# The low halves of q reach the attention operand by DMA, and the preparation of the weights is rewritten

## The chip, the cores and the metric

The kernel runs on one core of one Trainium2 chip. Its time is the device time of one execution in microseconds (us). The engines named below are TensorE (PE, with its weight loads as PEld), VectorE (DVE), ScalarE (ACT), GpSimd (POOL) and SyncE (SP), whose queue issues all DMAs here. A granted clock of 1.00 for TensorE means 2.4 GHz and 0.50 means 1.2 GHz.

## What is computed

The input x is 32 x 256 tokens of 128 numbers. Cut to what matters:

```python
q = relu((x @ Wq)) * SCALE; k = relu(x @ Wk); v = x @ Wv      # 64 heads of 64
kv    = einsum('bsid,bsjd->bsdj', k, v)
out   = einsum('bsid,bsdj->bsij', q, kv)
norm  = einsum('bsid,bsd->bsi', q, k.sum(axis=2))
x     = layernorm(x + (out / (norm + 1e-6)).reshape(b, s, 4096) @ Wo + bo)
h     = silu(fp4(x) @ fp4(w_gate).T) * (fp4(x) @ fp4(w_up).T)   # 352 wide
x     = layernorm(x + fp4(h) @ fp4(w_down).T)
```

`fp4` scales each block of 16 numbers by its largest magnitude over 6 and rounds to the grid 0, 0.5, 1, 1.5, 2, 3, 4, 6. In every token `kv` is summed over the same 64 heads for which `out` is taken, so the kernel needs, for each token, the sum of k over the heads and a 64 x 64 product of q with v.

## The kernel before

The 8192 tokens are worked in 64 tiles of 128. Matrix products are made of bf16 pairs: a float32 operand is split in a high half (its bf16 rounding) and a low half (what remains), and `three` adds high x high, high x low and low x high in PSUM. The high halves are written by ScalarE (`v_hi`, `q_hi`, `o_hi`), the low halves by VectorE (`v_lo`) and GpSimd (`q_lo`, `o_lo`).

There are 68 turns. In turn n the engines work on five tiles at once: the front (v, k and q of tile n), attention (`attend`, tile n-1), the output projection (`mid`, tile n-2), the first layernorm and gate/up (`back`, tile n-3), and the second layernorm (`end`, tile n-4). Each engine has its own order for a turn, written out by hand in `iteration(t)`, and engines meet only at semaphores. There is no scheduler: an instruction that waits holds up all that stands behind it on its engine.

TensorE's turn is: v 0 and 1, v 2 and 3, `x_transpose`, k 0 to 2, `h_transpose`, k 3, `down`, q 0, out 0, `k_sum`, out 1, `xq_transpose`, `gate_up`, q 1, out 2 and 3, q 2, out 4 and 5, output projection (`wo_part`, L408) 0 and 1, q 3, out 6, `wo_part` 2, out 7, `wo_part` 3 and 4. A chunk of v, k or q is 24 matmuls of 128 columns, an out group 24 of 66 columns. Three slots in PSUM of two banks each hold the chunks in the order of use (`USES`, `SLOT`); `wait_slot` lets a chunk in once its slot's earlier tenant has been read. By this order q 0 waits until VectorE has read k 1, and k 2 until it has read v 3.

`q_nat` holds q as it comes from VectorE (`q_scale`) with high and low halves; `q_bd` is the attention operand, block-diagonal, with two halves of 64 partitions for two parities. For each half (l = 0 high, l = 1 low) there are four blocks of 64 partitions x 2048 bf16: two change partitions and go by DMA (`q_move`), two stay on theirs (`q_stay`). Before, ScalarE copies three of those that stay (L563: the low one of partitions 0 to 63, and both high ones), and GpSimd the fourth (L1090, a multiplication by 1 from `consts`: the low one of partitions 64 to 127). All must be there before out 0:

```python
pe.wait_ge(s_qstay, t.n * 3)
pe.wait_ge(s_qstay_p, t.n)
pe.wait_ge(s_qbd, t.n * 64)
pe.wait_ge(s_vswap, t.n * 48)
```

SP's queue carries, per turn, three moves for the tile's o (`swap<-o_st`, `o_st<-o_st`, `o_st<-swap`, 512 KB each), three for its v (576 KB each), the four `q_move`s (256 KB each) and three small transfers. `wo_part(0)` waits for the last of the o moves.

After the tile's k has been summed over its chunks on VectorE (`k_add`, then three halvings `k_fold`, L733), `k_sum` (L447) on TensorE folds partitions, ScalarE copies the result to `ks`, and `q_scale` 0 starts from that. Between the second and the third `k_fold` VectorE has `norm_o(0)`, which waits for out 0. GpSimd's turn: `rstd_1` (two small operations for the first layernorm, L1067 and L1069), `q_stay`, `x_back`, `rstd_2`, then `q_lo` (L1051) 0 to 3 between `o_lo` (L1061) 0 to 7, `x_bias` and `h_back`. `x_one` (L820) on VectorE normalises with the result of `rstd_1`; it reads r1 and rs1, both in SBUF.

Ahead of the turns VectorE quantises w_gate and w_up (88 partitions x 1024) and w_down (128 x 352) by comparisons with the seven midpoints, and writes the low half of Wq (L708); GpSimd writes the low halves of Wv, Wk (L1030) and Wo (L1036).

## Time and profile before

| | |
|---|---|
| median of 3 runs | 2490.99 us (2480.89 to 2496.33) |
| the profiled execution | 2491.44 us, span 2489.7 us |
| mean granted TensorE clock | 0.941 |
| PE / PEld busy | 86% / 81% |
| DVE busy | 84% |
| POOL busy | 68% |
| ACT busy | 60% |
| DMA (mean of 16 engines) | 56.5% for the kernel's queue, 302.65 MB |

The profiled execution's own time is 0.45 us above the median, and 1.7 us of it lie outside the span. No engine is full, and the busy shares hardly change over the length of the run, so what limits the kernel is in how one turn closes on the next.

### The profile page before, as it was taken

The numbers are of one execution on the slowest core, as the hardware profiler recorded it, in microseconds if no ns is written. First come the engines' busy times: TensorE is split into PE (matmuls) and PEld (weight loads), VectorE is DVE, ScalarE is ACT, GpSimd is POOL, SyncE is SP. The second block draws the span as 40 slices with busy tenths as digits, with TensorE's granted clock in tenths as the row PEclk, the third lists the DMA queues.
The fourth block names the chain that finished last, engine by engine and source line by source line (L and its number), as shares of the span: only waits on it lengthen the run. The fifth ranks groups of instructions, "written<-read, shape, count | busy, mean of one in ns | idle before, by whom it ended". The sixth has DMA issues, their size and how long they took to land.

```text
span 2489.7 us, 88190 instructions
## 1 busy us (share of the span) xinstructions
PE 2144.2 (86%) x37963; PEld 2015.4 (81%) x37963; DVE 2088.1 (84%) x3943; ACT 1483.3 (60%) x2634; POOL 1702.6 (68%) x2068
## 2 busy tenths in 40 slices
PE   1788988988988988888898898898898898898875
PEld 1787978888888888888888888888888798898874
DVE  8679888888888888888888888888888988888874
ACT  3556656656656656656666666665665665665651
POOL 6566766766776776776776676676676676676673
PEclk9899999999999999999999999999999999999986
DMA  4456556556556556556656656655645655655651
GB/s 147 103 122 143 112 121 138 121 117 145 121 116 142 120 115 141 123 113 140 129 113 134 130 114 133 133 117 126 147 105 124 135 114 126 146 110 121 147 109 41
DMA packets 523211, 308.28 MB, mean 124 GB/s; under 512 B 275590, under 2 KB 497734, under 8 KB 522310
## 3 DMA queue, kind: packets, MB, share of 16 engines
q1 hardware_dynamic: 522822, 302.65, 56.5%
q8 instruction: 298, 4.88, 0.8%
q14 instruction: 91, 0.75, 0.1%
HBM read 17.38 MB, written 4.19 MB: 9 GB/s over the span
## 4 chain that ended last, share of the span: by engine, by line
PE 47%; DVE 32%; issue 10%; POOL 5%; ACT 5%; DMA 1%; SPq 0%; DVEq 0%; POOLq 0%; ACTq 0%
PE ps L408 13%; PE ps L361 10%; PE ps L362 9%; PE ps L363 9%; DVE k_acc L722 9%; DVE v_st L740 9%; DVE k_acc L733 3%; PE ps L462 3%; POOL o_st L1061 3%; POOL q_nat L1051 3%; ACT v_st L539 2%; PE ps L463 2%; DVE q L757 2%; PE ps L447 1%; DVE o L781 1%
## 5 line engine op out<-in xcount | busy, mean ns | idle before, releaser
L1061 POOL TENSOR_TENSOR o_st<-o,o_st 128x256 bf16<-128x256 f32 x1024 | 662.3, 680 | 50.9 <-ACT o_st L622 50.1
L1051 POOL TENSOR_TENSOR q_nat<-q,q_nat 128x512 bf16<-128x512 f32 x512 | 590.5, 1175 | 89.2 <-ACT q_nat L598 89.2
L622 ACT CAST o_st<-o 128x256 bf16<-128x256 f32 x1024 | 352.6, 403 | 285.2 <-DVE o L781 281.9
L361 PE MATMUL ps<-v_st,q_bd 128*128 128x66 bf16 x4096 | 465.9, 201 | 51.8 <-DVE o L781 25.1
L361 PEld LDWEIGHTS ps<-v_st,q_bd 128*128 128x128 bf16 x4096 | 423.4, 115 | 77.6 <-DVE o L781 41.4
L362 PE MATMUL ps<-v_st,q_bd 128*128 128x66 bf16 x4096 | 461.5, 200 | 0.0
L363 PE MATMUL ps<-v_st,q_bd 128*128 128x66 bf16 x4096 | 460.2, 199 | 0.0
L362 PEld LDWEIGHTS ps<-v_st,q_bd 128*128 128x128 bf16 x4096 | 424.8, 117 | 1.5 <-issue 0.4
L363 PEld LDWEIGHTS ps<-v_st,q_bd 128*128 128x128 bf16 x4096 | 422.3, 116 | 0.0
L598 ACT CAST q_nat<-q 128x512 bf16<-128x512 f32 x512 | 292.0, 618 | 210.6 <-DVE q L757 210.4
L361 PE MATMUL ps<-xT,w_q 128*128 128x128 bf16 x2048 | 377.5, 226 | 45.9 <-DVE k_acc L722 40.0
L408 PE MATMUL ps<-w_o,o_st 128*128 128x128 bf16 x6144 | 376.3, 220 | 4.0 <-DMA o_st<-swap 4.0
L362 PE MATMUL ps<-xT,w_q 128*128 128x128 bf16 x2048 | 374.9, 225 | 0.0
L363 PE MATMUL ps<-xT,w_q 128*128 128x128 bf16 x2048 | 373.0, 225 | 0.0
L757 DVE SCALAR_TENSOR_TENSOR q<-ps,ks 128x1024 f32<-128x1024 f32 x256 | 309.0, 1207 | 72.8 <-PE ps L363 55.8
L563 ACT COPY q_bd<-q_nat 64x2048 bf16<-64x2048 bf16 x192 | 363.6, 1894 | 7.7 <-POOL q_nat L1051 4.6
L361 PE MATMUL ps<-xT,w_v 128*128 128x128 bf16 x2048 | 351.4, 221 | 14.0 <-DVE v_st L740 12.2
L781 DVE TENSOR_TENSOR o<-ps,rec 128x512 f32<-128x512 f32 x512 | 337.4, 683 | 28.3 <-POOL o_st L1061 19.5
L740 DVE TENSOR_TENSOR v_st<-ps,v_st 128x1024 bf16<-128x1024 f32 x256 | 312.6, 1222 | 54.4 <-ACT v_st L539 45.1
L408 PEld LDWEIGHTS ps<-w_o,o_st 128*128 128x128 bf16 x6144 | 351.8, 114 | 5.0 <-DMA o_st<-swap 5.0
L362 PE MATMUL ps<-xT,w_v 128*128 128x128 bf16 x2048 | 351.3, 221 | 0.0
L363 PE MATMUL ps<-xT,w_v 128*128 128x128 bf16 x2048 | 351.3, 221 | 0.0
(133 smaller groups left out, 5710.0 us busy)
## 6 DMA issues: line engine op xcount, KB each, us to landing
q_bd<-q_nat SPq DMA_DIRECT2D x256, 256.0 KB, 3.9
swap<-v_st SPq DMA_DIRECT2D x64, 576.0 KB, 6.5
v_st<-v_st SPq DMA_DIRECT2D x64, 576.0 KB, 5.2
v_st<-swap SPq DMA_DIRECT2D x64, 576.0 KB, 5.4
swap<-o_st SPq DMA_DIRECT2D x64, 512.0 KB, 4.4
o_st<-o_st SPq DMA_DIRECT2D x64, 512.0 KB, 8.3
o_st<-swap SPq DMA_DIRECT2D x64, 512.0 KB, 5.9
x_in<-in_L_attn_x SPq DMA_DIRECT2D x64, 64.0 KB, 5.4
```

Of the source, the lines that this page charges most:

```text
L361: nc.tensor.matmul(dst, lhs(0), rhs(0), start=True, stop=False)
L362: nc.tensor.matmul(dst, lhs(0), rhs(1), start=False, stop=False)
L363: return nc.tensor.matmul(dst, lhs(1), rhs(0), start=False, stop=True)
L408: last = nc.tensor.matmul(Y, omat[t.par][:, lo, j // EB, :, j % EB], womat[:, lw, j, :], start=(j == 0 and k == 0), stop=(j == HALF - 1 an ...
L563: nc.scalar.copy(qbd[rows, l, :, a, e:e + HALF, :].rearrange("p k e s -> p k (e s)"), qnat[rows, l, a].rearrange("p k e s -> p k (e s)")). ...
L598: last = nc.scalar.copy(qnat[:, 0, a, :, c * EC:(c + 1) * EC, :], src[:, a])
L622: last = nc.scalar.copy(ost[1 - t.par][:, 0, :, a, g * G:(g + 1) * G, :], src[:, a])
L740: nc.vector.tensor_tensor(lo, slot_cols(("v", c)).rearrange("p e t -> p t e"), hi, ALU.subtract).then_inc(s_read["v"], 1)
L757: nc.vector.scalar_tensor_tensor(out=q32[:, c % QR, :].rearrange("p (e t) -> p e t", t=T), in0=slot_cols(("q", c)), scalar=0.0, in1=ks[:, ...
L781: nc.vector.tensor_tensor(o32[:, g % OR, :].rearrange("p (s b e) -> p s b e", b=2, e=HALF), slot_cols(("out", g))[:, :, 0:PW].rearrange("p ...
L1051: last = nc.gpsimd.tensor_tensor(qnat[:, 1, a, :, e, :], src[:, a], qnat[:, 0, a, :, e, :], ALU.subtract)
L1061: last = nc.gpsimd.tensor_tensor(lo[:, :, a], src[:, a], hi[:, :, a], ALU.subtract)
```

## The change

Both low blocks of q that stay now go by DMA, in a new `q_stay` on SP's queue, right behind the two low `q_move`s; ScalarE keeps the two high ones, and GpSimd has none. Out 0 waits for six transfers instead of four. The orders of the engines are edited in some places: on VectorE the first layernorm's statistics stand ahead of `v_lo(0)`, `x_one` ahead of `v_lo(3)`, `x_lo` behind `k_add(2)`, and `norm_o(6)` and `h_round` change places around `q_scale(3)`; on GpSimd `h_back` stands ahead of `o_lo(7)`; on ScalarE `h_step` stands three steps earlier.

The preparation: gate and up weights are quantised by the rounding trick that x and h already use (nine VectorE operations in place of sixteen), the low halves of Wv and Wk are written by VectorE, the quantising of w_down moves to the end of VectorE's turn 0 (its transposes and copies to turn 1), and the split of Wo moves into turn 0 (ScalarE behind `k_first`, GpSimd behind all that it has to do ahead of the first `q_lo`).

```diff
@@ sync @@
+            sp.dma_start(x_in[:, :], x_t[0:T, :]).then_inc(s_x, 16)
             for g, w in enumerate((w_gate, w_up)):
                 sp.dma_start(gu[0:WP, g], w.rearrange("(q p) k -> p q k", p=WP)).then_inc(s_fload, 16)
-            sp.dma_start(dn_raw, w_down).then_inc(s_fload, 16)
-            sp.dma_start(x_in[:, :], x_t[0:T, :]).then_inc(s_x, 16)
...
+            sp.dma_start(dn_raw, w_down).then_inc(s_dload, 16)
...
+            def q_stay(l, par):
+
+                rows, e = slice(par * 64, par * 64 + 64), par * HALF
+                sp.dma_start(qbd[rows, l, :, par, e:e + HALF, :].rearrange("p k e s -> p k (e s)"),
+                             qnat[rows, l, par].rearrange("p k e s -> p k (e s)")).then_inc(s_qbd, 16)
...
                     q_move(1, 0)
                     q_move(1, 1)
+                    q_stay(1, 0)
+                    q_stay(1, 1)
@@ tensor @@
-                    pe.wait_ge(s_qstay, t.n * 3)
-                    pe.wait_ge(s_qstay_p, t.n)
-                    pe.wait_ge(s_qbd, t.n * 64)
+                    pe.wait_ge(s_qstay, t.n * 2)
+                    pe.wait_ge(s_qbd, t.n * 96)
@@ scalar @@
-                q_stay(t, 1, 0)
+                if t.is_(0):
+                    weight_o_hi()
                 hq_copy(t)
-                q_stay(t, 0, 1)
-                q_stay(t, 0, 0)
+                q_stay(t, 1)
+                q_stay(t, 0)
                 k_sums(t)
+                if t.is_(1):
+                    down_weights()
...
                 o_hi(t, 4)
+                h_step(t)
                 o_hi(t, 5)
                 q_hi(t, 3)
                 o_hi(t, 6)
-                h_step(t)
                 o_hi(t, 7)
@@ vector @@
+            def quantise(raw, q, np_):
+                nb, w = raw.shape[1] // BLK, raw.shape[1]
+                raw, q, sc, rs = raw[0:np_], q[0:np_], w_sc[0:np_, 0:nb], w_sc[0:np_, 64:64 + nb]
                 link(nc.vector.tensor_reduce(sc, blocks(raw), AX.X, ALU.max, apply_absolute_value=True))
                 link(nc.vector.tensor_scalar(sc, sc, 1.0 / 6.0, 1e-12, ALU.mult, ALU.max))
                 link(nc.vector.reciprocal(rs, sc))
...
+                link(nc.vector.scalar_tensor_tensor(out=blocks(raw), in0=blocks(raw), scalar=BELOW_ONE,
+                                                    in1=per_block(rs, raw), op0=ALU.mult, op1=ALU.mult))
...
+                link(nc.vector.tensor_tensor(raw, q, raw, ALU.add))
+                link(nc.vector.tensor_tensor(q, raw, q, ALU.subtract))
                 nc.vector.tensor_tensor(blocks(q), blocks(q), per_block(sc, raw), ALU.mult).then_inc(s_wquant, 1)
...
+            for k in "vkq":
+                dve.wait_ge(s_whi[k], 1)
...
             def iteration(t):
                 residual_1(t)
-                v_lo(t, 0)
-                v_lo(t, 1)
                 stats_1(t)
                 before_mean_1(t)
+                v_lo(t, 0)
+                mean_1(t)
+                v_lo(t, 1)
                 v_lo(t, 2)
-                mean_1(t)
+                x_one(t)
                 v_lo(t, 3)
-                x_one(t)
                 k_add(t, 1)
                 x_max(t)
+                k_add(t, 2)
                 x_lo(t)
                 x_scale(t)
-                k_add(t, 2)
+                k_add(t, 3)
                 x_recip(t)
-                k_add(t, 3)
...
                 scale_o(t, 7)
-                h_round(t)
-                h_grid(t)
+                if t.is_(0):
+                    down_quantise()
@@ gpsimd @@
-            for k in "vk":
-                pool.wait_ge(s_whi[k], 1)
...
+            pool.wait_ge(s_whi["o"], 1)
+            nc.gpsimd.tensor_tensor(w_o[:, 1, :], stage["o"], w_o[:, 0, :], ALU.subtract).then_inc(s_wlo["o"], 1)
             pool.wait_ge(s_store, 16)
...
                 rstd_1(t)
-                q_stay(t)
                 x_back(t)
...
                 o_lo(t, 6)
+                h_back(t)
                 o_lo(t, 7)
-                h_back(t)
                 q_lo(t, 3)
```

GpSimd, from the last low half of q in one turn to the first in the next, before. `ve` and `rs` are `rstd_1` and `rstd_2`, `xq` is `x_back`.

```order
L1109 TENSOR_TENSOR h<-h,hsc 128x352
L1051 TENSOR_TENSOR q_nat<-q,q_nat 128x16x32 x2
L1067 TENSOR_TENSOR ve<-mv,consts 128x1
L1069 TENSOR_TENSOR rs<-ve,consts 128x1
L1090 TENSOR_TENSOR q_bd<-q_nat,consts 64x16x128
L1103 TENSOR_TENSOR xq<-xq,xsc 128x128
```

The same place after the change:

```order
L1072 TENSOR_TENSOR o_st<-o,o_st 128x8x32 x2
L1104 TENSOR_TENSOR h<-h,hsc 128x352
L1072 TENSOR_TENSOR o_st<-o,o_st 128x8x32 x2
L1062 TENSOR_TENSOR q_nat<-q,q_nat 128x16x32 x2
L1078 TENSOR_TENSOR ve<-mv,consts 128x1
L1080 TENSOR_TENSOR rs<-ve,consts 128x1
L1098 TENSOR_TENSOR xq<-xq,xsc 128x128
```

The operation on q_bd between `rs` and `xq` is gone, and `h` has moved up by one o_lo.

SP's queue at the start of a turn, before:

```order
L286 DMA swap<-o_st 64x16x256
L291 DMA q_bd<-q_nat 64x16x128 x2
L286 DMA swap<-v_st 64x2x2304
L286 DMA o_st<-o_st 64x16x256
L286 DMA v_st<-v_st 64x2x2304
L286 DMA o_st<-swap 64x16x256
```

And after:

```order
L285 DMA swap<-o_st 64x16x256
L290 DMA q_bd<-q_nat 64x16x128 x2
L296 DMA q_bd<-q_nat 64x16x128 x2
L285 DMA swap<-v_st 64x2x2304
L285 DMA o_st<-o_st 64x16x256
L285 DMA v_st<-v_st 64x2x2304
L285 DMA o_st<-swap 64x16x256
```

Two transfers of 256 KB now stand ahead of four of the moves of v and o.

VectorE at the start of a turn, before: the residual, the four `v_lo` (`v_st<-ps,v_st`) with the statistics between them, `x_one`, and the first `k_add`.

```order
L802 TENSOR_TENSOR r<-ps,x_res 128x128
L740 TENSOR_TENSOR v_st<-ps,v_st 128x128x8 x2
L807 BN_STATS st<-r 128x6
L740 TENSOR_TENSOR v_st<-ps,v_st 128x128x8
L815 BN_AGGR mv<-st 128x2
L740 TENSOR_TENSOR v_st<-ps,v_st 128x128x8
L820 SCALAR_TENSOR_TENSOR x<-r,mv,rs 128x128
L722 SCALAR_TENSOR_TENSOR k_acc<-ps,k_acc 128x1024
```

And after:

```order
L817 TENSOR_TENSOR r<-ps,x_res 128x128
L822 BN_STATS st<-r 128x6
L755 TENSOR_TENSOR v_st<-ps,v_st 128x128x8
L830 BN_AGGR mv<-st 128x2
L755 TENSOR_TENSOR v_st<-ps,v_st 128x128x8 x2
L835 SCALAR_TENSOR_TENSOR x<-r,mv,rs 128x128
L755 TENSOR_TENSOR v_st<-ps,v_st 128x128x8
L737 SCALAR_TENSOR_TENSOR k_acc<-ps,k_acc 128x1024
```

The normalisation `x` now stands ahead of the last `v_lo`.

## Rows read from the trace of the kernel before

**Rows 1.** The page, the chain that ended last: share of the span.

```profile
PE 47%; DVE 32%; issue 10%; POOL 5%; ACT 5%; DMA 1%; SPq 0%; DVEq 0%; POOLq 0%; ACTq 0%
```

**Rows 2.** The waits, whole run: us in total, times, longest.

```profile
PE ps L447 <- DVE k_acc L733: 134.0, 64, 2.6
```

**Rows 3.** The line L447: min/median/max ns, first and last start.

```profile
L447 PE MATMUL ps<-k_acc,both x128: 275/377/583, 69.7 to 2393.6; 128*128 128x128 f32 x128
```

**Rows 4.** ScalarE in order of time, ks of turn 2.

```profile
131.92 0.27 ACT L576 COPY ks<-ps 128x128 f32<-128x128 f32 x1 [2.02 <-PE ps L447]
```

**Rows 5.** VectorE in order of time, two turns: start, us, what.

```profile
1235.08 3.77 DVE L820 SCALAR_TENSOR_TENSOR x<-r,mv,rs 128x128 f32<-128x128 f32 x1
...
1271.88 3.77 DVE L820 SCALAR_TENSOR_TENSOR x<-r,mv,rs 128x128 f32<-128x128 f32 x1
```

**Rows 6.** Groups by line, whole run: busy us, mean ns | idle.

```profile
L820 DVE SCALAR_TENSOR_TENSOR x<-r,mv,rs 128x128 f32<-128x128 f32 x64 | 227.4, 3554 | 6.8 <-POOL rs L1069 6.8
```

**Rows 7.** GpSimd in order of time, the same turn.

```profile
1230.86 2.29 POOL L1051 TENSOR_TENSOR q_nat<-q,q_nat 128x512 bf16<-128x512 f32 x2
...
1234.38 0.55 POOL L1069 TENSOR_TENSOR rs<-ve,consts 128x1 f32<-128x1 f32 x1
1235.10 3.60 POOL L1090 TENSOR_TENSOR q_bd<-q_nat,consts 64x2048 bf16<-64x2048 bf16 x1 [0.17 <-POOL rs L1069]
...
1248.37 2.27 POOL L1051 TENSOR_TENSOR q_nat<-q,q_nat 128x512 bf16<-128x512 f32 x2 [0.24 <-ACT q_nat L598]
```

**Rows 8.** ScalarE in order of time, the same turn.

```profile
1237.36 0.59 ACT L570 COPY hqT<-ps 128x128 f32<-128x128 f32 x3 [0.21 <-PE ps L429]
1237.98 3.82 ACT L563 COPY q_bd<-q_nat 64x2048 bf16<-64x2048 bf16 x2
```

**Rows 9.** TensorE in order of time, the same turn.

```profile
1227.33 0.22 PE L361 MATMUL ps<-xT,w_v 128*128 128x128 bf16 x1
...
1241.85 0.22 PE L361 MATMUL ps<-v_st,q_bd 128*128 128x66 bf16 x1 [0.30 <-ACT q_bd L563]
...
1245.02 0.49 PE L447 MATMUL ps<-k_acc,both 128*128 128x128 f32 x2 [2.17 <-DVE k_acc L733]
...
1255.79 1.90 PE L408 MATMUL ps<-w_o,o_st 128*128 128x128 bf16 x31
```

**Rows 10.** One us: busy PE, PEld, DVE, ACT, POOL; clock; DMA, GB/s.

```profile
1246.00:1247.00 1.00, 0.88 (x13) 0.58 (x10) 1.00 (x2) 0.09 (x2) 0.04 (x1) 0.50 0.97 187
```

**Rows 11.** SP's queue in order of time, the same turn.

```profile
1233.17 1.31 SPq L291 DMA_DIRECT2D q_bd<-q_nat  x2
...
1243.58 0.59 SPq L286 DMA_DIRECT2D o_st<-swap  x1
```

**Rows 12.** DMA issues, 1225 to 1275 us: KB, us to landing.

```profile
o_st<-swap SPq DMA_DIRECT2D x1, 512.0 KB, 6.0
```

**Rows 13.** VectorE in order of time, the last turn with attention.

```profile
2419.97 0.35 DVE L820 SCALAR_TENSOR_TENSOR x<-r,mv,rs 128x128 f32<-128x128 f32 x1 [4.05 <-POOL rs L1069]
```

**Rows 14.** SP's queue in order of time, the end of turn 0.

```profile
82.68 3.93 SPq L291 DMA_DIRECT2D q_bd<-q_nat  x4
```

**Rows 15.** Stretches of 0.5 us there: clock, DMA share, GB/s.

```profile
84.00:84.50 0.50, 1.00 0.90 199
...
88.50:89.00 0.50, 1.00 0.84 172
```

**Rows 16.** VectorE in order of time, preparation.

```profile
8.57 1.22 DVE L687 TENSOR_TENSOR v_st<-v_st,o_st 88x1024 f32<-88x1024 f32 x1
...
13.78 11.22 DVE L693 SCALAR_TENSOR_TENSOR v_st<-v_st 88x1024 f32<-88x1024 f32 x3
...
57.29 3.49 DVE L740 TENSOR_TENSOR v_st<-ps,v_st 128x1024 bf16<-128x1024 f32 x3
```

**Rows 17.** GpSimd in order of time, preparation.

```profile
46.33 8.78 POOL L1036 TENSOR_TENSOR w_o<-q_nat,w_o 128x4096 bf16<-128x4096 f32 x1 [6.82 <-ACT w_o L524]
```

**Rows 18.** DMA issues, first 62 us: KB, us to landing.

```profile
v_st<-in_L_attn_Wq SPq DMA_DIRECT2D x1, 2048.0 KB, 17.6
```

More of the change, by code:

```diff
@@ L616, in o_hi @@
                     return
+                if g == 0 and t.is_(2):
+                    act.wait_ge(s_wlo["o"], 1)
                 if g == 0 and t.back:
@@ new lines, in quantise @@
+                nc.vector.tensor_tensor(blocks(q), blocks(q), per_block(sc, raw), ALU.mult).then_inc(s_wquant, 1)
+            dve.wait_ge(s_fload, 32)
+            quantise(gu_raw, gu_q, WP)
+            dve.wait_ge(s_xhi, 1)
+            nc.vector.tensor_tensor(xT[0][:, 1, :], TB1[:, 0:T], xT[0][:, 0, :], ALU.subtract).then_inc(s_xlo, 1)
+            for k in "vkq":
+                dve.wait_ge(s_whi[k], 1)
+                for hh in range(2):
+                    hi, lo = (wmat[k][:, l].rearrange("p e (h m) -> p e h m", h=2)[:, :, hh] for l in range(2))
+                    if k == "q":
+                        last = nc.vector.scalar_tensor_tensor(out=lo, in0=split_src["q"][:, :, hh], scalar=SCALE, in1=hi,
+                                                              op0=ALU.mult, op1=ALU.subtract)
+                    else:
+                        last = nc.vector.tensor_tensor(lo, split_src[k][:, :, hh], hi, ALU.subtract)
+                last.then_inc(s_wlo[k], 1)
@@ L996, in iteration @@
                 y(t)
-                norm_o(t, 6)
                 scale_o(t, 5)
                 q_scale(t, 3)
+                h_round(t)
+                norm_o(t, 6)
                 norm_o(t, 7)
```

105 lines of the change are left out of this document (32 added, 73 removed).

## The prediction

> **What bounds the kernel now.** I read the chain of work that ended last first [rows 1]: 47% of the span is TensorE, 32% VectorE, and 10% "issue", time in which an engine waited for nothing that the profile shows. The waits then name where the two engines meet: before `k_sum` TensorE stands 134.0 us in 64 turns for VectorE's last `k_fold` [rows 2]. `k_sum` is therefore the clock of a turn. Its first start is 69.7 us and its last 2393.6 us [rows 3]; that of turn 2 lies half a microsecond ahead of the ScalarE copy that reads it, at 131.4 us [rows 4]. From there to the last, 61 turns take 2262 us, 37.08 us each. The two turns shown are 36.80 us apart (1271.88 less 1235.08) [rows 5].
>
> Why VectorE is late stands in the same rows: `x_one`, 128 x 128, takes 3.77 us [rows 5]. Over the run it has a mean of 3554 ns [rows 6], against 0.35 us in the last turn with attention, where it came ahead of GpSimd's copy [rows 13]. In the ordinary turn GpSimd's q_stay starts at 1235.10 us, 0.02 us behind `x_one`, and ends at 1238.70; `x_one` ends 0.15 us after that [rows 5, 7]. So VectorE stands still for 3.4 us in each turn while GpSimd copies from SBUF. The Trainium skill, page "SBUF — State Buffer", section "SBUF: two separate sides", says that a VectorE operation with two SBUF inputs and a GpSimd operation take a shared pair of ports as an exclusive lock. By that rule the copy holds `x_one` for its whole length, and the trace agrees.
>
> Then the clock: behind the 2.17 us of idling before `k_sum` [rows 9] TensorE's granted clock is 0.50, its 1.2 GHz level, in the microsecond from 1246 us [rows 10]. A mean of 0.941 for the run means that 0.118 of the time, 4.4 us a turn, is spent at that level; half of it, 2.2 us, is lost to TensorE. I take 1.7 for this turn.
>
> **The change in the steady turn.** I count from a `k_sum`, at 0.
>
> GpSimd's q_stay (3.60 us) goes. Nothing of GpSimd waits behind it that is urgent, so the gain is `x_one`: 3.77 to 0.35 us, 3.4 us off VectorE's path to the next `k_sum`. If nothing else were late, the turn would be 33.4 us.
>
> What is late next, on four paths:
>
> (a) GpSimd. Its first `q_lo` starts at 3.35 (1248.37 less 1245.02) and its last ends at 24.9 (1230.86 + 2.29 + 36.80, less 1245.02) [rows 7, 9]. In between it works nearly without a gap, and the change takes nothing from that stretch; `h_back` moves within it. I take 24.7. `rstd_1` stands behind it and takes 0.8 (its second part ends at 1234.93) [rows 7]; before, this was hidden, since `x_one` came behind all four `v_lo`. Now `x_one` stands ahead of `v_lo(3)`, so the chain is: 24.7, `rstd_1` 25.6, `x_one` 25.95, `v_lo(3)` with its 1024 columns (1.22 us each, the starts a little closer) [rows 16] 27.1. k 2 needs the slot that this frees. Behind k 2 come `h_transpose` (together 1.8 us), `hq_copy` 0.6, and ScalarE's two high copies, 3.82 us [rows 8]: 33.3. Out 0 starts then, takes 1.0, and `norm_o(0)` and the last `k_fold` 0.5 more: the next `k_sum` at 34.9.
>
> (b) ScalarE. It loses one copy of 1.9 us, but that one lay in its wait for `h_transpose`; the other two still start right behind `hq_copy`, as before at 1237.98 [rows 8]. From v 0 to the end of the copies are 14.5 us (1227.33 to 1241.80) [rows 8, 9]. So the removed copy is worth nothing, and TensorE's wait for ScalarE before out 0 (0.30 us in this turn) becomes longer, since q 0 comes earlier. v 0 starts at 19.1 after the `k_sum` now (1227.33 + 36.80 less 1245.02), and at 17.4 if the clock stays up: the next `k_sum` by this path at 35.1 or 33.4.
>
> (c) The low halves by DMA. SP issues the two moves at 1233.17, as GpSimd ends, 1.31 us for both [rows 11]. Now it issues four. Four moves of this size in a row stand at the end of turn 0: issued from 82.68, their data flows from 84.0 to 89.2, so 1.3 us each and 6.5 us in all [rows 14, 15]. From 24.7 that gives 31.2, ahead of ScalarE's 33.3. Two fewer waits on engines, one longer on the DMA, 2.1 us of cover.
>
> (d) The moves behind them in the queue. v's and o's moves come later by the two added transfers, 2.6 us. The last of o is issued at 35.4 (1243.58 + 36.80 less 1245.02) and takes 6.0 [rows 11, 12]: 41.4, then 44.0. `wo_part(0)` reads it 10.8 after the next `k_sum` [rows 9], so at 47.6 before, and at 45.7 now, or 44.2 with the clock up. A margin of 6.2 us shrinks to 0.2 to 1.7.
>
> The cost of the added transfers can be seen in another way. The Trainium skill, page "DMA: Bandwidth & Descriptors", section "Specifications", asks for at least 512 bytes per piece for full rate; these pieces are 256 bytes, so by it each move costs about twice its bytes, some 2.6 us as an estimate. The sum of (d) would then be 46.6, and the o moves would be the bound. What the trace has for pieces of this size speaks against it: 199 and 172 GB/s in [rows 15]. I take 1.3 us each, with 2.1 as the upper bound.
>
> I take 34.9 us for the turn, from (a), with (b) at 33.4 to 35.1 beside it. 61 turns give 61 x (37.08 - 34.9) = 133 us. Turn 2 has no `x_one` but three copies on ScalarE in a row; it loses one, 2 us. The last turn with attention has the short `x_one` already and gains nothing.
>
> **The preparation.** VectorE's first `v_lo` is at 57.29 us [rows 16]. Now the gate and up weights take seven operations of 1024 columns at 1.22 us, two small ones of 0.4, from about 5 us on: 14.6, with x 14.9. The old ones of this size took 3.7 each where GpSimd split Wv and Wk beside them (11.22 us for three) [rows 16]; GpSimd has nothing there now. Six operations of 2048 columns follow, at twice 1.22 or less: 29.5. Wq lands at 3.5 + 17.6 = 21.1 [rows 18] and ScalarE needs 3.6 for it, which gives 24.7 and with the last two 29.6. So 27.7 us come forward. From that goes what is put into turn 0: the split of Wo, 8.78 us on GpSimd [rows 17], now falls on `k_fold`, which reads SBUF on both inputs, so between 0 and 7 us. I take 6, since ScalarE's copy of Wo ends about where `k_fold` begins. The quantising of w_down (seven operations of 352 columns, some 0.5 us each by 1.22 x 352/1024 and the fixed part) goes ahead of turn 1's `v_lo`, which had 2 us of idling: 3.5, up to 7 if `q_lo` blocks it. 27.7 - 6 - 3.5 = 18 (14 to 26). The small edits (`norm_o(6)` behind `q_scale(3)`, `h_step` earlier, `x_lo` later) I cost at nothing: they move idling of VectorE within the second half of the turn, where GpSimd sets the pace; were they on the path, 0.3 us a turn either way.
>
> The sum against the profiled execution: 2491.4 - 133 - 2 - 18 = **2338 us**. It is 0.45 us above the median of the runs, so the same number stands for the median.
>
> **The rivals.**
>
> TensorE sets the pace. If the clock stays up and `rstd_1` comes sooner than I think, path (b) gives 33.4 to 33.6: 61 x 3.55 = 217, and with 20 for the rest **2254 us**. For it: the chain is mostly TensorE. Against it: GpSimd's stretch is full.
>
> The DMA sets the pace. With 2.1 us for each added move the o moves land at 45.6 and `wo_part(0)` waits: 45.6 - 9.6 = 36.0 a turn, 66 us less and 20 for the rest, **2405 us**. For it: the queue carries them in front of four larger moves, and the margin is small. Against it: the rate in [rows 15].
>
> Slower. The same mechanism at a higher price: a copy whose source and destination are the same 64 partitions has no row of this size alone. If the two cost 8 us together, o lands at 49.4 and the turn is 38.6: 61 x 1.5 = 93 more, less 20, **2564 us**. It decides from 6.9 us for both (41.4 + 6.9 - 10.8 = 37.5). Nothing in the rows is that slow.
>
> It doesn't do what it says. If `x_one` is slow for another reason than GpSimd's copy, 3.5 us stay, and only the preparation is won: about **2470 us**. Against it: [rows 13].
>
> **How the numbers follow.** My forecast has 0.62, TensorE's pace 0.15, the DMA's 0.15, slower 0.04, nothing but preparation 0.04. The forecast's own range is 2289 to 2387 (34.1 to 35.7 a turn). To hold 8 in 10 it must reach to both neighbours: 2250 to 2410. Faster by over 1% (about what a measurement of this kernel can tell from no change) takes in the first three, 0.92; within 1% 0.05, slower by over 1% 0.03.
>
> **What would show it.** `x_one` at 0.35 us in all turns; TensorE's wait before `k_sum` under 1 us a turn, and a longer one before out 0 that ScalarE ends, not a DMA; a short wait of k 2 for `v_lo(3)`; mean granted clock over 0.941; the last move of o landing 2 to 3 us later in the turn, with no wait of `wo_part`; the first `v_lo` near 30 us and a `k_fold` of some us in turn 0. I am wrong if TensorE's idling is short and a turn is under 34 us, or if `wo_part` or out 0 waits for a DMA.

## The result, and the profile after

The changed kernel takes 2428.84 us (median of 4 runs, 2424.65 to 2429.46), the kernel before 2493.66 us (4 runs, 2480.89 to 2498.93). The ratio is 0.9744, with a 95% interval of 0.9704 to 0.9784: 2.6% faster, where 6% was forecast, and above the range. The profiled execution took 2429.46 us, 62 us less than that of before; its span is 2427.7 us and its mean granted clock 0.946 (before 0.941).

The chain that ended last, on the page of after:

```profile
PE 51%; POOL 13%; ACT 12%; DVE 9%; DMA 7%; issue 5%; SPq 2%; ACTq 0%; DVEq 0%; POOLq 0%
```

Against [rows 1], VectorE's share has gone from 32% to 9%, as it had to if `x_one` was the brake. But 7% of the chain is now DMA, of which [rows 1] had 1%.

TensorE's waits after, over the run (us in total, times, longest us):

```profile
PE ps L368 <- issue: 60.0, 21, 9.8
PE ps L368 <- ACT q_bd L571: 52.8, 42, 2.1
PE ps L368 <- DVE o L796: 47.0, 89, 2.6
PE ps L451 <- DVE k_acc L748: 37.2, 64, 8.4
...
PE ps L414 <- DMA o_st<-swap: 16.2, 13, 6.0
```

The wait before `k_sum` fell from 134.0 us [rows 2] to 37.2, 8.4 of them in turn 0. In its place TensorE waits ahead of out 0 (L368 is the first matmul of chunks and out groups): 42 times for ScalarE's copies, which was foreseen, and 21 times for "issue", which is a wait that the trace gives no engine for. What ends these is shown below. The longest of the 21, 9.8 us, is out 0 of the last turn with attention.

VectorE's normalisations after, by line (busy us, mean ns):

```profile
L905 DVE SCALAR_TENSOR_TENSOR y_out<-r,mv,rs 128x128 f32<-128x128 f32 x64 | 92.1, 1439 | 0.9 <-POOL rs L1080 0.9
L835 DVE SCALAR_TENSOR_TENSOR x<-r,mv,rs 128x128 f32<-128x128 f32 x64 | 22.4, 350 | 19.3 <-POOL rs L1080 13.6
```

`x_one` has a mean of 350 ns where [rows 6] had 3554: the stall is gone in all 64 turns. Still, `k_sum` gives only this (min/median/max ns, first and last start):

```profile
L451 PE MATMUL ps<-k_acc,both x128: 275/377/582, 51.0 to 2327.6; 128*128 128x128 f32 x128
```

Its last start is 66 us earlier than in [rows 3], its first 18.7. ScalarE's copy to `ks`, which follows each `k_sum`, starts at 85.77 us in turn 1 (96.52 before), at 118.45 in turn 2 (131.92 [rows 4]). From there the 61 turns take 36.22 us each instead of 37.08: 52 us won, where 133 were forecast. Behind the last `k_sum` the changed kernel takes 4 us more than before (2427.7 - 2327.6 against 2489.7 - 2393.6).

**Where the turn closes now.** One turn of after, in the order of its end. SP's queue:

```profile
1431.59 0.59 SPq L285 DMA_DIRECT2D swap<-o_st  x1
1433.79 1.44 SPq L290 DMA_DIRECT2D q_bd<-q_nat  x2
1435.27 2.88 SPq L296 DMA_DIRECT2D q_bd<-q_nat  x2
1438.26 1.68 SPq L285 DMA_DIRECT2D swap<-v_st  x1
1439.99 0.73 SPq L285 DMA_DIRECT2D o_st<-o_st  x1
```

ScalarE, and TensorE behind it:

```profile
1438.61 3.82 ACT L571 COPY q_bd<-q_nat 64x2048 bf16<-64x2048 bf16 x2
```

```profile
1443.64 0.22 PE L368 MATMUL ps<-v_st,q_bd 128*128 128x66 bf16 x1 [2.28 <-issue]
```

ScalarE's copies end at 1442.43. Out 0 starts 1.2 us later. By the queue's rows of that turn the slowest of its six q transfers took 6.9 us to land; the last one is issued near 1436.7, and 1436.7 + 6.9 is 1443.6, where out 0 starts. Over the run (landing: us from issue):

```profile
L290 SPq DMA_DIRECT2D q_bd<-q_nat x256: 590/668/2058, 66.8 to 2352.6; - x128
...
DMA to landing us min/median/max: 3.2/4.1/5.4
```

```profile
L296 SPq DMA_DIRECT2D q_bd<-q_nat x128: 674/1376/2797, 70.9 to 2354.9; - x128
...
DMA to landing us min/median/max: 4.0/5.3/7.9
```

L290 is `q_move`, L296 the new `q_stay`. The issue of a new transfer takes 1376 ns by the median, twice that of the old, and it lands 5.3 us later, up to 7.9. The stretches of that turn show why (us; the last two columns are the DMA engines' share and GB/s):

```profile
1434.00:1436.00 2.00, 2.00 (x39) 2.00 (x37) 1.88 (x3) 1.73 (x3) 0.53 (x1) 1.00 0.93 206
1436.00:1438.00 2.00, 2.00 (x36) 1.99 (x34) 1.74 (x4) 0.01 (x1) 0.00 (x0) 1.00 0.98 208
...
1440.00:1442.00 2.00, 1.36 (x25) 1.19 (x22) 1.97 (x7) 1.98 (x2) 0.00 (x0) 1.00 1.06 208
...
1447.00:1448.00 1.00, 0.96 (x14) 0.67 (x11) 1.00 (x3) 0.00 (x1) 0.00 (x0) 0.50 0.70 156
```

The DMA engines are nearly full from 1434 to 1442, at a share of 0.93 and above in the stretches shown: a move of o (512 KB) ahead, four transfers of q (1024 KB), a move of v (576 KB) behind. And TensorE's idling before out 0 is followed by a granted clock of 0.50 (1.2 GHz) from 1444 to 1450 us, as the idling before `k_sum` was in [rows 10].

I call the time from the end of ScalarE's copies to the next copy of `ks` the tail of a turn, and count turns 3 to 62. Before, the tail is 3.80 us, which holds the wait for the last `k_fold`. After, it is 2.75 on average and 2.01 at the least; in 24 of 60 turns it is over 2.4.

**A second stall.** In 14 of 60 turns (6 before) `y_out`, the normalisation of the second layernorm, takes 4.2 us. VectorE and GpSimd in such a turn of after:

```profile
491.83 4.22 DVE L905 SCALAR_TENSOR_TENSOR y_out<-r,mv,rs 128x128 f32<-128x128 f32 x1
495.97 0.68 DVE L796 TENSOR_TENSOR o<-ps,rec 128x512 f32<-128x512 f32 x1
```

```profile
489.79 2.59 POOL L1072 TENSOR_TENSOR o_st<-o,o_st 128x256 bf16<-128x256 f32 x4
492.32 2.33 POOL L1062 TENSOR_TENSOR q_nat<-q,q_nat 128x512 bf16<-128x512 f32 x2
494.57 1.33 POOL L1072 TENSOR_TENSOR o_st<-o,o_st 128x256 bf16<-128x256 f32 x2
```

GpSimd works without a gap to 495.90; `y_out` ends at 496.05, the same 0.15 us behind as `x_one` in [rows 5, 7]. The 14 turns take 37.67 us on average, the other 46 take 35.83. In most of the others `y_out` takes 0.70 us, which is not its free length either (342 ns with one input in PSUM, below): it is held there by one `o_lo`, and ends 0.15 us behind it. The Trainium skill, page "SBUF — State Buffer", section "SBUF: two separate sides", has the lock held for one whole instruction. By that alone `y_out` could have started between two instructions of the chain. In these 14 turns it did not: it waited through five of them.

### The profile page after: what moved, and what is told of

It is laid out like the page before. It is cut to its first block, busy times and chain, and to the rows that moved or that the text cites. A ratio compares the mean times of both kernels' runs of the same rounds, so it can differ in the third digit from the quotient of the medians.

```text
span 2427.7 us, 87981 instructions
## 1 busy us (share of the span) xinstructions
PE 2123.7 (87%) x37963; PEld 2015.4 (83%) x37963; DVE 1907.6 (79%) x3933; ACT 1375.6 (57%) x2570; POOL 1447.1 (60%) x2000
## 4 chain that ended last, share of the span: by engine, by line
PE 51%; POOL 13%; ACT 12%; DVE 9%; DMA 7%; issue 5%; SPq 2%; ACTq 0%; DVEq 0%; POOLq 0%
PE ps L368 12%; PE ps L414 11%; PE ps L370 11%; PE ps L369 11%; ACT q_bd L571 8%; POOL o_st L1072 6%; POOL q_nat L1062 6%; DMA o_st<-o_st 4%; DVE q L772 3%; DMA o_st<-swap 3%; DVE o L796 2%; PE ps L466 2%; PE ps L451 1%; SPq L296 1%; ACT q_nat L604 1%
## 5 line engine op out<-in xcount | busy, mean ns | idle before, releaser
L368 PE MATMUL ps<-v_st,q_bd 128*128 128x66 bf16 x4096 | 471.7, 202 | 159.9 <-issue 60.0
L368 PEld LDWEIGHTS ps<-v_st,q_bd 128*128 128x128 bf16 x4096 | 426.7, 116 | 187.4 <-DVE o L796 64.2
L369 PE MATMUL ps<-v_st,q_bd 128*128 128x66 bf16 x4096 | 469.0, 201 | 0.0
L370 PE MATMUL ps<-v_st,q_bd 128*128 128x66 bf16 x4096 | 467.9, 200 | 0.0
L1098 POOL TENSOR_TENSOR xq<-xq,xsc 128x128 f32<-128x128 f32 x64 | 25.9, 404 | 669.2 <-DVE xq L881 669.2
L414 PE MATMUL ps<-w_o,o_st 128*128 128x128 bf16 x6144 | 388.9, 223 | 16.5 <-DMA o_st<-swap 16.2
L414 PEld LDWEIGHTS ps<-w_o,o_st 128*128 128x128 bf16 x6144 | 363.4, 115 | 19.5 <-DMA o_st<-swap 19.0
L796 DVE TENSOR_TENSOR o<-ps,rec 128x512 f32<-128x512 f32 x512 | 341.7, 682 | 39.1 <-POOL o_st L1072 33.4
L368 PE MATMUL ps<-xT,w_q 128*128 128x128 bf16 x2048 | 364.1, 222 | 6.0 <-DVE q L772 5.9
L368 PE MATMUL ps<-xT,w_v 128*128 128x128 bf16 x2048 | 352.8, 221 | 15.9 <-DVE v_st L755 9.8
L369 PE MATMUL ps<-xT,w_q 128*128 128x128 bf16 x2048 | 363.4, 221 | 0.0
L370 PE MATMUL ps<-xT,w_q 128*128 128x128 bf16 x2048 | 363.1, 221 | 0.0
L368 PE MATMUL ps<-xT,w_k 128*128 128x128 bf16 x2048 | 353.3, 220 | 1.8 <-DVE v_st L755 1.8
L369 PE MATMUL ps<-xT,w_k 128*128 128x128 bf16 x2048 | 353.1, 220 | 0.0
```

The source lines that it names most:

```text
L368: nc.tensor.matmul(dst, lhs(0), rhs(0), start=True, stop=False)
L369: nc.tensor.matmul(dst, lhs(0), rhs(1), start=False, stop=False)
L370: return nc.tensor.matmul(dst, lhs(1), rhs(0), start=False, stop=True)
L414: last = nc.tensor.matmul(Y, omat[t.par][:, lo, j // EB, :, j % EB], womat[:, lw, j, :], start=(j == 0 and k == 0), stop=(j == HALF - 1 an ...
L796: nc.vector.tensor_tensor(o32[:, g % OR, :].rearrange("p (s b e) -> p s b e", b=2, e=HALF), slot_cols(("out", g))[:, :, 0:PW].rearrange("p ...
```

## The experiments

Each was timed beside the kernel before on the same chip (medians 2488.62, 2486.29 and 2488.87 us for the three batches). "Turn" is the mean of turns 3 to 62 in us, "long" the number of these 60 turns in which `y_out` takes 4.2 us, "late" that of tails over 2.4 us. Between runs of different batches a distance in us is rough: by the ratios, each times 2490, the 59, 43, 80 and 64 us named below are 57, 38, 78 and 59.

| run | median us | ratio, 95% interval | turn | long | late | clock |
|---|---|---|---|---|---|---|
| the changed kernel | 2428.84 | 0.9744 (0.9704 to 0.9784) | 36.26 | 14 | 24 | 0.946 |
| e1_low_q_by_dma_alone | 2426.98 | 0.9752 (0.9705 to 0.9800) | 35.98 | 16 | 18 | 0.953 |
| e2_all_but_low_q | 2369.49 | 0.9515 (0.9486 to 0.9544) | 35.07 | 16 | 0 | 0.973 |
| e3_r1_in_psum | 2357.90 | 0.9469 (0.9439 to 0.9499) | 35.04 | 11 | 0 | 0.972 |
| e4_scalar_keeps_its_low | 2376.05 | 0.9554 (0.9514 to 0.9594) | 35.47 | 21 | 2 | 0.965 |
| e5_r2_in_psum | 2385.80 | 0.9593 (0.9556 to 0.9631) | 35.54 | 0 | 28 | 0.957 |
| e6_v_move_held | 2545.27 | 1.0232 (1.0197 to 1.0267) | 37.91 | 24 | 1 | 0.946 |
| e9_all_but_low_q_r2_psum | 2305.67 | 0.9280 (0.9253 to 0.9307) | 34.19 | 0 | 0 | 0.983 |
| e10_x_one_ahead_alone | 2444.67 | 0.9846 (0.9810 to 0.9881) | 36.42 | 21 | 0 | 0.964 |
| e11_wo_split_late | 2308.33 | 0.9277 (0.9252 to 0.9301) | 34.17 | 0 | 0 | 0.979 |
| e12_before_r1_r2_psum | 2328.25 | 0.9363 (0.9341 to 0.9384) | 34.45 | 0 | 0 | 0.980 |
| e13_statistics_and_x_one_ahead | 2397.2 | 0.9613 (0.9577 to 0.9650) | 35.68 | 26 | 0 | 0.969 |

**The transfers alone.** The kernel before with both low blocks that stay moved by DMA, and nothing else of the change.

```diff
+                    q_stay(1, 0)
+                    q_stay(1, 1)
...
-                    pe.wait_ge(s_qstay, t.n * 3)
-                    pe.wait_ge(s_qstay_p, t.n)
-                    pe.wait_ge(s_qbd, t.n * 64)
+                    pe.wait_ge(s_qstay, t.n * 2)
+                    pe.wait_ge(s_qbd, t.n * 96)
...
-                q_stay(t, 1, 0)
...
-                q_stay(t)
```

> The kernel before, with one part of the change: both low blocks of q that stay go by DMA, ScalarE and GpSimd lose theirs, nothing else is edited. My theory: VectorE's x_one falls from 3.77 to 0.35 us in all turns and this alone gives what the turns gained (0.86 us each), so 2491 less 45 to 75: 2415 to 2445 us, with the landing of four transfers late in some turns as in the changed kernel. Rival: the turns gained by the reordering on VectorE and GpSimd, and the transfers give nothing or cost: 2480 us or more.

2426.98 us, the same as the whole change. `x_one` is at 343 ns, and TensorE again waits ahead of out 0 for no engine (48.9 us, 19 times). The late landing comes with the transfers, not with the new order. This run has the old preparation, which costs some 10 us; that it is no slower than the changed kernel means that with the transfers in, the new orders bring nothing that can be seen.

**The rest alone.** The changed kernel with the copies where they were: ScalarE has three, GpSimd its multiplication behind `rstd_1`, SP four transfers.

```diff
-                    q_stay(1, 0)
-                    q_stay(1, 1)
...
+                q_stay(t, 1, 0)
                 hq_copy(t)
...
                 rstd_1(t)
+                q_stay(t)
                 x_back(t)
```

> The changed kernel with the low blocks of q put back: one on ScalarE, one on GpSimd, four transfers; preparation and orders stay changed. My theory: x_one is held by GpSimd's copy again (3.77 us), now in front of the last v_lo, so the turns are 37.1 us or longer, and only the 10.7 us of the preparation remain: 2475 to 2500 us. Rival (the orders made the gain): 2430 to 2445 us.

2369.49 us: 59 us faster than with the transfers, and far below what my theory gave, which had `x_one` held as before. My theory of this run fell. `x_one` in it (min/median/max ns):

```profile
L835 DVE SCALAR_TENSOR_TENSOR x<-r,mv,rs x64: 350/352/3356, 148.2 to 2338.0; 128x128 f32<-128x128 f32 x64
```

One turn of it, VectorE and then GpSimd:

```profile
1315.37 0.35 DVE L835 SCALAR_TENSOR_TENSOR x<-r,mv,rs 128x128 f32<-128x128 f32 x1 [0.54 <-POOL rs L1080]
```

```profile
1314.79 0.55 POOL L1080 TENSOR_TENSOR rs<-ve,consts 128x1 f32<-128x1 f32 x1
1315.51 3.68 POOL L1101 TENSOR_TENSOR q_bd<-q_nat,consts 64x2048 bf16<-64x2048 bf16 x1 [0.17 <-POOL rs L1080]
```

GpSimd's copy is still there and as long as in [rows 7]. But `x_one`, ahead of `v_lo(3)`, now waits for `rs` itself and starts 0.14 us ahead of the copy, and is done. In the kernel before its recorded start lay ahead of the copy's too, but by 0.02 us [rows 5, 7] (0.02 to 0.03 in all 60 turns in which it was held). It is [rows 13] in nearly every turn: 61 of 64; in the other three it starts 0.4 us or more behind the copy's start and is held. The order alone, with `x_one` and the statistics moved up, removes the stall that the two transfers were to remove.

**One input in PSUM.** The kernel before, with r1 in a free quarter of a PSUM bank instead of SBUF, and the waits that keep TensorE and VectorE apart on that bank.

```diff
-        r1, x1, xm, xq = (sb(v, [T, DIM]) for v in ("r1", "x1", "xm", "xq"))
+        x1, xm, xq = (sb(v, [T, DIM]) for v in ("x1", "xm", "xq"))
...
+        r1 = TB0[:, 3 * T:3 * T + DIM]
```

> The kernel before, with one edit: r1 lies in PSUM, in columns of TB0 that nothing else uses, so that x_one has one SBUF input. GpSimd's copy of 3.60 us, ScalarE's three and the four transfers stay. If x_one is slow because two SBUF inputs meet GpSimd's reads, it takes 0.35 us now, VectorE gets its 3.4 us without a single added transfer, TensorE's tail behind ScalarE's copies has no late landing, and a turn is 35.2 to 36.0 us: 2375 to 2425 us. If GpSimd's copy slows VectorE in another way, x_one stays near 3.7 us and the time near 2491.

2357.90 us, 5.3% faster, with the old order, copies and preparation, and 17 us below the range expected. In its trace `x_one` reads PSUM and takes 342 ns, with GpSimd's copy (3599 ns) beside it:

```profile
L825 DVE SCALAR_TENSOR_TENSOR x<-ps,mv,rs 128x128 f32<-128x128 f32 x64 | 21.9, 342 | 6.8 <-POOL rs L1074 6.8
L1095 POOL TENSOR_TENSOR q_bd<-q_nat,consts 64x2048 bf16<-64x2048 bf16 x64 | 230.3, 3599 | 11.4 <-POOL rs L1074 10.8 <-POOL q_nat L1056 0.5
```

The added waits have not moved `x_one` out of the copy's way, as the order did above. One turn of it, VectorE and then GpSimd:

```profile
1171.78 0.34 DVE L825 SCALAR_TENSOR_TENSOR x<-ps,mv,rs 128x128 f32<-128x128 f32 x1
```

```profile
1171.80 3.60 POOL L1095 TENSOR_TENSOR q_bd<-q_nat,consts 64x2048 bf16<-64x2048 bf16 x1 [0.17 <-POOL rs L1074]
```

It starts 0.02 us ahead of the copy, as in [rows 5, 7], and is not held. So the stall hangs on the second SBUF input of VectorE's operation: the cause that the prediction named is shown, and the transfers are not needed against it.

**Five transfers.** The changed kernel with ScalarE keeping its low block; only GpSimd's goes by DMA.

```diff
-                    q_stay(1, 0)
                     q_stay(1, 1)
...
+                q_stay(t, 1, 0)
                 hq_copy(t)
```

> The changed kernel, but ScalarE copies its low block as before, ahead of the hidden representation's copy, where it lay in a wait; only GpSimd's block goes by DMA: five transfers instead of six. Theory of late landing: out 0 waited for the transfers in 24 of 60 turns, 0.7 us a turn in the mean; with one fewer (1.3 us) most of that goes and ScalarE's copy costs nothing: 2385 to 2410 us. Rival (the landing doesn't depend on the last transfer, or ScalarE's copy now delays the other two): 2425 us or more.

2376.05 us, 9 us below the range expected. One transfer less takes the late tails from 24 to 2, and ScalarE's copy costs nothing that can be seen, as (b) had it. It is the sixth transfer that is on the path.

**y_out.** The changed kernel with r2 left in PSUM.

```diff
-        r2, y_out = (sb(v, [T, DIM]) for v in ("r2", "y_out"))
+        y_out = sb("y_out", [T, DIM])
...
+        r2 = DN
...
+                    pe.wait_ge(s_yo, t.e)
```

> The changed kernel, with the residual r2 of the second layernorm left in the PSUM block that the down projection wrote, so that y_out has one SBUF input instead of two (the next user of that block waits for y_out). In the changed kernel y_out is held for 4.2 us in 14 of 60 turns, and these turns take 37.7 us against 35.8. Theory that the held y_out is a cost of its own: y_out takes about 0.35 us in all turns, and 14 x 1.85 = 26 us go: about 2403. Rival, that the long y_out turns are long for another reason (GpSimd runs back to back there because it is late anyway): y_out is short and the time stays within 5 us of the changed kernel's 2428. Out 0 still waits for the low blocks in a third of the turns under both.

2385.80 us, 43 us less than the changed kernel, more than the 26 expected: `y_out` is at 342 ns throughout, and the clock rises from 0.946 to 0.957. The held `y_out` is a cost of its own. Out 0 is late about as often as in the changed kernel (28 and 24).

**The v move held back.** The changed kernel, with SP waiting ahead of v's first move until q has landed.

```diff
                     sp.wait_ge(s_read["v"], chunks)
+                    if t.attend:
+                        sp.wait_ge(s_qbd, t.n * 96)
                     move(v4[t.par], vsw, s_vswap, vm[0], 0)
```

> The changed kernel, with SP waiting, ahead of the first move of v (576 KB), until all six transfers of q have landed. Theory A, the low blocks land late because the next move shares the DMA engines with them: with it held back they land some 1 us earlier, out 0 waits in fewer than 10 of 60 turns, and the turn gets 0.3 to 0.5 us shorter, about 2405; the three moves of v and the last of o come later by some 3 us, which costs something only if the output projection then waits. Theory B, the low blocks are late because four transfers of 256-byte pieces take as long as they take from the last q_lo on: out 0 still waits as often, and the o moves behind come later, so the time is 2428 or above, up to 2470 if the output projection waits each turn.

2545.27 us, slower than before the change. The longest landing of L296 falls from 7.9 to 6.2 us, and the last low transfer lands 8.2 us behind the last `q_lo` instead of 9.0, so the v move does share the engines with q, but for 0.8 us only. Late tails fall from 24 to 1 for another reason as well: ScalarE's copies end 35.9 us behind the copy of `ks`, where the changed kernel has 33.5. The turn is not shorter. TensorE's waits in this run:

```profile
PE ps L416 <- DMA o_st<-swap: 145.2, 63, 6.0
PE ps L370 <- ACT q_bd L573: 69.0, 60, 1.6
PE ps L453 <- DVE k_acc L750: 37.4, 64, 8.4
```

L416 is `wo_part`. Behind the held v move the second and third moves of o are late, and the output projection waits 2.3 us in every turn. Neither theory had the size; the mechanism is that of the prediction's slower rival. With six transfers of q the queue was late for out 0 in the one order and for `wo_part` in the other.

**Both together.** The rest alone, and r2 in PSUM.

> The changed kernel without its new transfers (both low blocks copied by ScalarE and GpSimd as in the kernel before, measured at 2369 us) and with r2 in PSUM as in the run of that name. There y_out was held in 16 of 60 turns, 37.05 us against 34.35. Theory that a held y_out delays all behind it on VectorE: 16 x 2.7 = 43 us less, about 2326, all turns near 34.4. Rival, that these turns are long because GpSimd is late: no more than 5 us less, about 2365. If only the stall itself is lost and made up in part later in the turn, between the two, 2345.

2305.67 us, 7.2% faster than before and some 5% faster than the changed kernel (0.9280 over 0.9744); the best run here. Beside the rest alone, on another chip, 64 us came from freeing `y_out`, more than the 43 of the first theory: the clock, at 0.983, adds its part. Half of the turns are at 34.15 us or less, the minimum is 34.12.

**One line of order.** The kernel before with `x_one` ahead of `v_lo(3)`.

```diff
-                v_lo(t, 3)
                 x_one(t)
+                v_lo(t, 3)
```

> The kernel before with one line moved: x_one ahead of v_lo(3) on VectorE. No transfer is added, GpSimd and ScalarE keep their copies, and the preparation is the old one. Theory that the order alone frees x_one, because it then waits for rstd_1 and starts ahead of GpSimd's copy: x_one takes 0.35 us in nearly all turns, and the turn comes to about 35.1 us as where r1 lies in PSUM, 2358 to 2380 us. The distance to the run of the changed kernel without its transfers (2369) is then what the preparation and the small edits are worth, 10 to 20 us by the 18 forecast. Rival, that the other edits of VectorE's order are needed (statistics ahead of v_lo(0)): x_one still starts behind the copy and takes 3.7 us, about 2475 to 2490.

2444.67 us: between the two. `x_one` is at 352 ns in all turns, so its stall is gone, but the one line gives less than the two transfers alone did (2426.98). The waits show what took its place:

```profile
POOL ve L1067 <- DVE mv L815: 75.6, 62, 7.0
DVE x L820 <- POOL rs L1069: 63.8, 64, 4.0
```

The second was 6.8 us in the kernel before, the first 65.8. The old order has the mean only behind `v_lo(2)`. `rstd_1` waits for it, `x_one` for `rstd_1`, and `v_lo(3)`, k 2 and ScalarE's copies stand behind: these end 34.35 us behind the copy of `ks`, against 33.29 before. 21 turns have a held `y_out`.

**The statistics as well.** The same, and the first layernorm's statistics ahead of `v_lo(0)`.

```diff
+                stats_1(t)
+                before_mean_1(t)
                 v_lo(t, 0)
+                mean_1(t)
                 v_lo(t, 1)
-                stats_1(t)
-                before_mean_1(t)
                 v_lo(t, 2)
-                mean_1(t)
```

> The kernel before with x_one ahead of v_lo(3), as in the run with that line alone (2445 us), and the statistics of the first layernorm ahead of v_lo(0). With x_one alone moved, rstd_1 waited 75.6 us for the mean and x_one 63.8 us for rstd_1, about 1 us a turn, which held v_lo(3). Theory that this wait ate half of what the freed x_one gave: with the statistics ahead x_one starts 0.8 us behind the last q_lo instead of 1.9, the turn is shorter by about 1 us, and the total 2375 to 2390; the distance to the run without the new transfers (2369) is the worth of the preparation and the remaining small edits. Rival, that the preparation is what separates 2445 from 2369: within 10 us of 2445.

2397.2 us, 47 us less than with the one line, 7 above the range of the theory. The wait for `rs` is 8.0 us, and a turn with a short `y_out` takes 34.52 us. 26 turns have a held one, and `x_one` is still held in eight (mean of all 640 ns). To the 2369 of the rest alone 28 us are left: 10 are the preparation (the copy of `ks` in turn 1 at 99.48 and 89.77 us), and the rest goes with ten more held `y_out`; whether a small edit of order avoids these or they fall by chance, I can't tell.

**Both residuals in PSUM, nothing else.** Orders, copies and preparation of before.

> The kernel before with both residuals, r1 and r2, left in PSUM, so that neither x_one nor y_out has two SBUF inputs. Orders, transfers and preparation are those of before. With r1 alone it took 2358 us, and y_out was held in 11 of 60 turns, 36.79 us against 34.65 in the others. Theory that the lock is all that matters in the steady turn: all turns at 34.4 to 34.7, about 2330, and what is left to the 2306 of the run without the new transfers and with r2 in PSUM is the preparation and the small edits of order (some 10 and 15 us). Rival, that freeing y_out in this order brings nothing, since GpSimd's copy then meets another operation of VectorE: no better than 2350.

2328.25 us, 6.4% faster with two buffers moved, and as expected. Both normalisations in its trace:

```profile
L827 DVE SCALAR_TENSOR_TENSOR x<-ps,mv,rs 128x128 f32<-128x128 f32 x64 | 21.9, 342 | 6.8 <-POOL rs L1076 6.8
L897 DVE SCALAR_TENSOR_TENSOR y_out<-ps,mv,rs 128x128 f32<-128x128 f32 x64 | 21.9, 342 | 0.9 <-POOL rs L1076 0.9
```

To the best run 23 us are left: 8 in the preparation (the second `ks` at 96.48 and 88.30), and 0.26 us a turn, 16 in all, in the order.

**The split of Wo.** The best run, with GpSimd's low half of Wo at the end of its turn 0.

```diff
-            pool.wait_ge(s_whi["o"], 1)
-            nc.gpsimd.tensor_tensor(w_o[:, 1, :], stage["o"], w_o[:, 0, :], ALU.subtract).then_inc(s_wlo["o"], 1)
...
                 q_lo(t, 3)
+                if t.is_(0):
+                    pool.wait_ge(s_whi["o"], 1)
+                    nc.gpsimd.tensor_tensor(w_o[:, 1, :], stage["o"], w_o[:, 0, :], ALU.subtract).then_inc(s_wlo["o"], 1)
+                    pool.wait_ge(s_wlo["o"], 1)
```

> The run without the new transfers and with r2 in PSUM (2306 us), with GpSimd's low half of Wo (7.93 us) moved from ahead of the first q_lo to the end of its turn 0, where it has nothing to do for some 15 us. Theory that the split holds the three k_folds of turn 0 (8.58 us instead of 1.3), and that the 10 us of idling it leaves on TensorE bring the granted clock down to 0.50 for the q chunks behind it: the k_folds take 1.3 us, the first k_sum comes at about 45.5 us instead of 52.6, and the q chunks may run at full clock, another 3 to 5 us; the second k_sum 7 to 12 us earlier, the total near 2297. Rival, that the split only moves its cost (on to w_down's quantising or the residual work of turn 1): the second k_sum less than 3 us earlier, total 2303 to 2306.

2308.33 us: nothing gained. VectorE in turn 0 of this run, then GpSimd:

```profile
43.60 1.48 DVE L750 TENSOR_TENSOR k_acc<-k_acc 128x512 f32<-128x512 f32 x3
...
63.08 8.13 DVE L705 TENSOR_TENSOR o_st<-o_st 128x352 f32<-128x352 f32 x1
71.24 3.81 DVE L706 TENSOR_TENSOR o_st<-o_st 128x352 f32<-128x352 f32 x1
```

```profile
62.62 8.21 POOL L1144 TENSOR_TENSOR w_o<-o_st,w_o 128x4096 bf16<-128x4096 f32 x1
70.90 3.76 POOL L1101 TENSOR_TENSOR q_bd<-q_nat,consts 64x2048 bf16<-64x2048 bf16 x1
```

The theory was right on the `k_fold`s: 1.48 us, and the first `ks` 7.5 us earlier (45.66, was 53.14). The rival was right on the rest: the same lock now holds two operations of w_down's quantising, for 8.13 us behind the split and 3.81 behind the copy of q (in the best run only the copy held one, 3.81 us), and the second `ks` comes at 90.97 instead of 88.30. The theory on the clock failed: the `q_scale`s of turn 0 show how far the q chunks are apart, and here, without the stall, two of their three distances are 4.06 us, where the best run, with the stall, has 4.06 once and 2.83 twice.

## Why the prediction was wrong

**The first link was right.** That `x_one` is held by GpSimd's copy, what frees it (0.35 us in all turns), and that `k_sum` then no longer waits for VectorE, came out as forecast, and the run with r1 in PSUM shows the lock by itself. So was (a) nearly: in the best run the last `q_lo` ends at 23.5, `x_one` starts at 24.3 and the copies end at 32.2 us behind the copy of `ks` (behind `k_sum`, from which the prediction counts, it is some 0.6 more). With nothing else late the turn is 34.2 us; the 34.9 of the forecast was not too low.

**The step that failed is (c).** It let the last low transfer land 6.5 us behind the last `q_lo`, at 31.2 us, from 1.3 us for each of four at 200 GB/s, with 2.1 us of cover. Out of the traces, as means of turns 3 to 62, in us behind the copy of `ks`:

| run, low transfers | last `q_lo` ends | last q lands | between | ScalarE's copies end |
|---|---|---|---|---|
| the kernel before, 2 | 24.6 | 30.4 | 5.7 | 33.3 |
| e4_scalar_keeps_its_low, 3 | 24.5 | 32.3 | 7.7 | 33.4 |
| the changed kernel, 4 | 24.7 | 33.7 | 9.0 | 33.5 |
| e6_v_move_held, 4 | 27.2 | 35.4 | 8.2 | 35.9 |

The four took 9.0 us and not 6.5, and the cover was gone. The rate was right (206 and 208 GB/s in the stretches); what was mis-sized is the way to the landing of the last. The rows it came from were misread in part: of the four transfers of [rows 14] the two low ones had to wait for the last `q_lo`, were issued at 84.98 and 85.61, and the last landed at 89.86, 0.7 us behind the end of the flow. They also had nothing ahead of them in the queue, whereas here a move of o is issued 2.2 us ahead and the moves of v and o follow. The kernel before had the better row. Its landings:

```profile
L291 SPq DMA_DIRECT2D q_bd<-q_nat x256: 590/630/996, 82.7 to 2419.8; - x128
...
DMA to landing us min/median/max: 3.2/3.9/7.1
```

The later of its two low transfers lands 5.1 us after its issue on average, and the two already need 5.7 us in a steady turn; with twice 1.3 that makes 8.3, which leaves 0.4 us of cover. The remaining 0.7 go with the v move, as the run that holds it back shows (8.2); what the move of o ahead costs no run has by itself. The last q transfer lands up to 7.9 us after its issue, and in 24 of 60 turns the tail is late.

Taking the transfers out is worth 59 us beside a held `y_out` (2428.84 and 2369.49) and 80 without (2385.80 and 2305.67). That is most of the 91 us by which the prediction was off, and it means that the change's main edit costs more than it gives once `x_one` is placed well. By the trace of the changed kernel the 91 us are 61 x (36.22 - 34.9) = 80 in the turns, 7 in the preparation and 4 behind the last `k_sum`, where out 0 of the last turn with attention waits 9.8 us; the prediction had this last term at nothing.

**Not foreseen: `y_out`.** The prediction weighed the lock for the one operation that was held in the turn it looked at. `y_out` reads two SBUF inputs as well, and takes 4.2 us in 6 turns before, 14 after. It is worth 43 us in the changed kernel, 64 without the transfers. The kernel before showed it in the maximum of its line, beside a median of 703 ns:

```profile
L890 DVE SCALAR_TENSOR_TENSOR y_out<-r,mv,rs x64: 341/703/4220, 218.0 to 2487.3; 128x128 f32<-128x128 f32 x64
```

**The clock.** The forecast had part of the 1.2 GHz time vanish with the wait before `k_sum`; it went from 0.941 to 0.946, since the idling before out 0 is followed by the 1.2 GHz level as the idling before `k_sum` was. At 0.983, in the best run, 2 x 0.017 x 2302 = 78 us are spent at that level, in the changed kernel 2 x 0.054 x 2428 = 262.

**(b)** was right: ScalarE's copy is worth nothing that the run with five transfers could show, and TensorE's wait for ScalarE ahead of out 0 grew from 23.9 to 52.8 us in all. **(d)** was right in its margin, which was thin: from the landing of the last o move to `wo_part(0)` it is 1.0 us on average (5.6 before), `wo_part` waits 16.2 us in 13 turns, where the prediction had no wait, and 145.2 as soon as the queue is delayed by one wait more. By the estimate of 2.6 us for each added move that the prediction drew from the Trainium skill, page "DMA: Bandwidth & Descriptors", section "Specifications", it would have waited in every turn; the trace does not agree, with pieces of 256 bytes carried beside larger ones at 208 GB/s.

**The preparation** gave 10.7 us and not 18 at the second `k_sum`. The first `v_lo` starts at 30.24 us (29.6 forecast), 27.05 earlier. Against that stand the split of Wo on the `k_fold`s, 8.40 us for three where the run with the split moved has 1.48, so 6.9 (6 forecast), and w_down: 6.0 us long, but in a gap of VectorE that was there before, so that turn 1's `v_lo` follows the last `q_scale` of turn 0 3.8 us later than it did (3.5 forecast). Two terms were left out. The q chunks of turn 0 come 4.06 us apart three times, in the kernel before once, with 2.83 twice: 2.4 us. TensorE's granted clock is 0.50 behind them up to 64 us, but the best run has the same stall of the `k_fold`s and 4.06 only once, so the stall doesn't explain it, and the cause stays open. Smaller delays ahead of the `k_fold`s and in turn 1 make 3.2. 27.05 - 6.9 - 3.8 - 2.4 - 3.2 is 10.75. Turn 2 gave 2.7 (2 forecast).

**The rivals.** The result lies nearest to "the DMA sets the pace" (2405), and in kind it was that, but at another place: out 0 waits for q, not `wo_part` for o. That its number is near is luck: its turn of 36.0 takes 9.6 us from `k_sum` to `wo_part(0)`, where (d) and the slower rival take 10.8 [rows 9], and with 10.8 it gives 34.8 us and no wait. Its chance of 0.15 was too low for an edit that puts two transfers on a queue and makes a wait of TensorE hang on the last of them.

What stays open: how much of the 59 to 80 us is the waiting itself and how much the clock behind it. Of the 1.35 us a turn between the two runs with r2 in PSUM (35.54 and 34.19) 0.59 lie in the tail; the other 0.76 lie ahead of the end of ScalarE's copies, and nothing here splits them. Open too is why a `y_out` gets in between two GpSimd operations in some turns (0.70 us) and not in others. In most turns of both kinds it starts 0.11 to 0.16 us behind an `o_lo`, with GpSimd's next operation close behind.
